# Gathers of a graph network in four forms: the same rows read as floats, as integer words, with an index bound, and as bytes

## What is computed

```python
def _gine_conv(x, src, dst, e, W1, b1, W2, b2):
    msg = relu(x[src] + e)                                # e: [E, 96], from the edge's weight
    agg = segment_sum(msg, dst, num_segments=N)
    h = relu((x + agg) @ W1 + b1)
    return relu(h @ W2 + b2)
# layer 0: two _gine_conv one after the other, then x = layernorm(x + h)
# layer 1: message = concat([x[row], x[col], edge_feat]), then relu(message @ W + b),
#          batch statistics over the edges, segment_sum by col; x = layernorm(x + agg + node_feat)
```

## Time and profile before

| | us |
|---|---|
| timed runs, median of 2 (12,207.96 and 12,225.78) | 12,216.87 |
| span of the profiled execution (the page gives no further time for it) | 14,691.4 |
| busy in it: PE / PEld | 9,543.3 / 6,790.2 |
| busy in it: POOL | 9,148.4 |
| busy in it: DVE / ACT | 7,533.7 / 4,925.7 |

### The profile page before, as it was taken

One profiled execution on the slowest core, in us unless ns is written; L12 is line 12 of the kernel. 1 busy time (PEld: TensorE's weight loads), 2 busy tenths in 40 slices (PEclk: granted clock), 3 DMA queues, 4 the chain that ended last, 5 costly groups with the idle time before them and its releaser, 6 DMA issues. The chain is left out here.

```text
span 14691.4 us, 164775 instructions
## 1 busy us (share of the span) xinstructions
PE 9543.3 (65%) x34164; PEld 6790.2 (46%) x34164; DVE 7533.7 (51%) x15604; ACT 4925.7 (34%) x11020; POOL 9148.4 (62%) x9725
## 2 busy tenths in 40 slices
PE   3666666666666677777777777766555555555556
PEld 2544444444444444455555555544444444444444
DVE  3433434334333444455555555556666666666666
ACT  2322222222222333333333333333333333333333
POOL 6466666666666566666666666656666666666665
PEclk9999999999999655555555555555555555555555
DMA  3111111111111211122222222211122222212122
GB/s 80 32 40 40 40 41 40 41 40 40 41 40 40 54 42 43 43 47 45 46 46 46 47 46 45 47 43 41 42 45 43 44 43 44 44 44 44 43 44 47
DMA packets 580837, 647.55 MB, mean 44 GB/s; under 512 B 411208, under 2 KB 411689, under 8 KB 579722
## 3 DMA queue, kind: packets, MB, share of 16 engines
q0 software_dynamic: 309504, 476.02, 15.5%
q1 hardware_dynamic: 219142, 139.69, 3.9%
q10 hardware_dynamic: 51712, 27.54, 0.7%
HBM read 604.68 MB, written 39.43 MB: 44 GB/s over the span
## 5 line engine op out<-in xcount | busy, mean ns | idle before, releaser
L1309 PE MATMUL ps_pre<-w_e,conv_hid 97*128 97x96 f32 x12896 | 3268.4, 433 | 2144.1 <-DVE conv_part L600 1554.4
L1309 PEld LDWEIGHTS ps_pre<-w_e,conv_hid 97*128 97x128 f32 x12896 | 2873.9, 326 | 2886.6 <-issue 2393.8
L1309 PE MATMUL ps_pre<-last_w_q,last_hid 128*128 128x96 f32 x6448 | 1627.8, 432 | 1540.8 <-issue 935.3
L1309 PEld LDWEIGHTS ps_pre<-last_w_q,last_hid 128*128 128x128 f32 x6448 | 1440.1, 327 | 1928.3 <-issue 1605.6
L264 POOL DMA_INDIRECT early_got<-in_x_rows,early_idx x1612 | 1524.3, 946 | 960.5 <-issue 439.0
L264 POOL DMA_INDIRECT early_got<-h_rows,early_idx x1612 | 1520.8, 943 | 944.2 <-issue 478.3
L264 POOL DMA_INDIRECT early_got<-p_rows,early_idx x1612 | 1520.4, 943 | 926.6 <-issue 463.3
L264 POOL DMA_INDIRECT last_got<-p_rows,early_idx x1612 | 1520.8, 943 | 905.0 <-issue 430.5
L264 POOL DMA_INDIRECT conv_got<-h_rows,early_idx x1612 | 1520.8, 943 | 884.0 <-issue 435.6
L264 POOL DMA_INDIRECT conv_got<-in_x_rows,early_idx x1612 | 1520.7, 943 | 853.1 <-issue 447.1
L582 ACT ACTIVATE conv_part<-ps_pre 128x384 bf16<-128x384 f32 x1736 | 816.0, 470 | 3676.9 <-DVE ps_pre L641 2405.4
(11 more groups left out here) (255 smaller groups left out, 10572.7 us busy)
## 6 DMA issues: line engine op xcount, KB each, us to landing
conv_row<-ea_parts SPq DMA_DIRECT2D x372, 84.5 KB
last_row<-ea_parts SPq DMA_DIRECT2D x372, 84.5 KB
early_got<-in_x_rows,early_idx POOLq DMA_INDIRECT x1612
conv_got<-in_x_rows,early_idx POOLq DMA_INDIRECT x1612
early_got<-h_rows,early_idx POOLq DMA_INDIRECT x1612
conv_got<-h_rows,early_idx POOLq DMA_INDIRECT x1612
early_got<-p_rows,early_idx POOLq DMA_INDIRECT x1612
last_got<-p_rows,early_idx POOLq DMA_INDIRECT x1612
```

Source lines behind the costliest of these rows:

```text
L1309: mm = pe.matmul(ps["pre"][q % 2][:, t * C:(t + 1) * C], hid[q % 2][0:P if last else C1, t * P:(t + 1) * P], w_q[j % U][:, c * C:(c + 1) * ...
```

## The change

Three more functions stand beside `gather`. `gather_words` reads both the table and the destination as 32-bit integers; `gather_checked` is the plain form with a bound on the index, 12,799, beyond which a row would be skipped without an error; `gather_bytes` reads both sides as bytes, so that a row is 384 elements rather than 96. Each moves the same 384 bytes a row. In `gpsimd_windows` slab j of a round is gathered by form[j]: slab 0 as before, slab 1 as words, slab 2 with the bound, slab 3 as bytes. `Preparation.gathers` keeps the plain form.

```diff
+U8 = mybir.dt.uint8
...
         def gather(gp, table, to, index, t, sem):
             gp.indirect_dma_start(to[:, t * C:(t + 1) * C], None, table, bass.IndirectOffsetOnAxis(index[:, t:t + 1], 0)).then_inc(sem, 16)
+
+        def gather_words(gp, table, to, index, t, sem):
+            gp.indirect_dma_start(to[:, t * C:(t + 1) * C].bitcast(I32), None, table.bitcast(I32),
+                                  bass.IndirectOffsetOnAxis(index[:, t:t + 1], 0)).then_inc(sem, 16)
+
+        def gather_checked(gp, table, to, index, t, sem):
+            gp.indirect_dma_start(to[:, t * C:(t + 1) * C], None, table, bass.IndirectOffsetOnAxis(index[:, t:t + 1], 0),
+                                  bounds_check=NPAD - 1, oob_is_err=False).then_inc(sem, 16)
+
+        def gather_bytes(gp, table, to, index, t, sem):
+            gp.indirect_dma_start(to[:, t * C:(t + 1) * C].bitcast(U8), None, table.bitcast(U8),
+                                  bass.IndirectOffsetOnAxis(index[:, t:t + 1], 0)).then_inc(sem, 16)
+
+        form = [gather, gather_words, gather_checked, gather_bytes]
...
                                 for i, t in enumerate(range(*group_tiles(g))):
                                     if near:
                                         close(k, NC_ * j + g, i)
-                                    gather(gp, table, got[j], idx[j], t, s[f"got{j}{g}"])
+                                    form[j](gp, table, got[j], idx[j], t, s[f"got{j}{g}"])
```

## The result

The changed kernel took 12,338.32 us (two runs, 12,336.70 and 12,339.93) against 12,216.87: a ratio of 1.0103, interval [1.0084, 1.0122]. That is 121 us more, inside the 2% band around no change and inside the forecast's range, but beyond the noise of the runs: the interval does not hold 1. What can be compared is every duration.

The account below looks back on a forecast made before the run. POOL's gather rate was taken as the bound: 9,672 x 1.248 = 12,071 us floor, 146 below the median. Words, bytes and bound added 0 + 0 + 0, so 12,217 us was forecast, range 12,110 to 12,640.

Parts of the forecast that it names:

- the MOVE: POOL's queue, ahead of each bounded gather: instruction putting the bound in a register, taken as covered by 1.25 us spacing, 0.
- rival 4: All gathers: forms differ by less than 0.1 us, nothing measurable; inside the forecast's 12,120 to 12,320, no chance of its own.
- the pauses: Whole core idle between gathers: 2,571 us of POOL pauses and waits, taken as belonging to the profiled execution, not timed runs.
- the distance of 1.248 us: POOL, start to start of gathers: 0.94 us busy plus 0.30 issue; 9,672 of them give a floor of 12,071 us.
- five waits of 221 us: POOL: 87.8 us in the first pass, 20.6, 23.6 and 17.1 around pass changes, 72 after the last gather.
- Rival 2: Byte gathers: 384-element rows are dearer; 12,580 us with a 0.15 us surcharge, 19,070 if rows are cut in four; chance 0.07.
- rival 3: One new gather form takes a shorter path, 0.84 us rather than 0.944, saving 242 us, time 11,975; chance 0.12.
- rival 1: Slab 2's 2,418 gathers: the explicit bound costs POOL 0.10 to 0.31 us each, 12,580 at the middle price; chance 0.18.
- The 0.10 us taken from the row of MEMSET: Bounded gathers: price if the comparison is a pass of its own over 128 lanes on POOL, +242 us.
- the rule of the Trainium skill: Bounded gathers: about 102 cycles per index fetched by itself, 10.9 us a gather, some 26,000 us; given no chance.
- the sum line: Whole kernel: form costs 0 + 0 + 0, profiled execution unchanged at 14,691 us, timed median 12,217 us.
- 7.4 ns a row: POOL's gather: 944 ns for 128 rows read as work going by rows, used to price dearer forms.

Follow-up runs that it names:

- e12: Kernel before with all four slabs bounded, bound loaded in a register once a pass, on a chip without pauses: 12,713.34 us against 12,210.33, ratio 1.0412.
- e11: Kernel before with slabs of 96 rows plain, 96 bounded, 32 plain, 32 bounded after each pass's first round: 11,887.02 us against 12,209.87, ratio 0.9736, one run.
- e10: Kernel before, all gathers plain, without the throttle waits of `close`, on a chip without pauses: 12,208.15 us against 12,209.87, ratio 0.9999.
- e2: Kernel before with words in slabs 0 and 2, bytes in 1 and 3, no bound, on a chip with pauses: 14,878.17 us against 14,877.60, ratio 1.0001.
- e3: Kernel before with all four slabs bounded, bound loaded in a register once a pass, on a chip with pauses: 14,859.60 us against 14,877.60, ratio 0.9988.
- e1: Kernel before with all four slabs bounded, a MOVE ahead of each bounded gather, on a chip with pauses: 14,974.24 us against 14,877.60, ratio 1.0066.
- e5: Kernel before with slabs of 128 rows plain, 128 bounded, 64 plain, 64 bounded after each pass's first round: 14,906.61 us against 14,843.74, ratio 1.0042, one run.
- e6: Kernel before with slab 0 plain, others bounded by 12,799 with error, 6,400 and 1, after each pass's first round: 14,938.88 us against 14,843.74, ratio 1.0064, one run.
- e7: Kernel before with all four slabs bounded, a MOVE per bounded gather, repeated on another chip with pauses: 14,928.95 us against 14,843.74, ratio 1.0057.
- e0: Kernel before, unchanged, with a new profile, on a chip with pauses: 14,882.43 us against 14,877.60, ratio 1.0003.

## Why the prediction was right

GpSimd's rate as the limit was right, and so were the costs of 0 for words, bytes and the MOVE. The price of 0 for the index bound was not, and the time lies inside the range because the range reached to 12,640 for a dearer bound. What came is rival 4, forms that differ by less than 0.1 us; but 12,338 is 18 us above the 12,320 given for it, and it does differ from no change beyond the noise.

- **The bound was POOL's rate, and a cost there is paid in full.** Right, and shown: 121 of 128 us in the change, 503 of 510 in e12, 323 of 335 in e11. The argument from the two times, that a run of 12,217 us leaves no room for the pauses, was what carried it. One step beside it was off: the distance of 1.248 us was taken to be 1% too long, because five waits of 221 us didn't fit beside it. Without pauses the distance is the same 1.249 us (e10); it is the wait of 87.8 us that isn't there, and the two changes of pass take 56 to 61 us.
- **Words and bytes cost nothing.** Right: 943 to 945 ns in the profile after and in e2, 32 packets a gather as before. Rival 2 (bytes dearer) and rival 3 (a shorter path) did not come.
- **The bound costs nothing.** Off in size: it costs 53 ns a gather, +128 us by the sum, where the forecast took 0 and rival 1 began at +0.10 us. This is the whole distance between 12,217 and 12,338. The reason given, one fixed routine in which the bound is a value, was wrong: a gather without a bound is shorter by 53 ns. The 0.10 us taken from the row of MEMSET lay above it, but that is luck: nothing shows that the comparison is a pass over the lanes. The range's lower end, 12,110, was said to take in -0.05 us on one form; that would be 12,096. What the rule of the Trainium skill in "GPSIMD Engine Reference", section "Performance pitfalls for Q7 kernels", would have made of an index fetched by itself, an estimated 10.9 us, is not seen in any form.
- **The MOVE is covered.** Right, by e3 and e12 against e1 and the change: 997 ns with it and without, the same gap, and no time without pauses. On chips with pauses 9 to 14 ns are paid for each (e1, e5, e6, e7), which the step did not foresee.
- **The pauses belong to the profiled execution.** As it was meant, of that one execution, this step failed. They are there in ten timed runs of e0 (14,878 to 14,888 us), and the profile after has none: its span is 12,334.9 us where the sum line said 14,691 unchanged, and its windows hold 291 gathers where the signs said 245 to 248. The prediction had two numbers, 14,691 and 12,217, and put the difference on profiling, when another reading, two chips, was open. Whether recording makes the pauses on some chips remains open, as said at e0. The step did no harm only because the result was measured without pauses. On one with them the same change would have paid less: e1 and e7, with four times as many bounded gathers, 0.6%.
- **7.4 ns a row.** This failed too. 863 of 944 ns are there with 32 rows. Rivals 1 and 2 priced their dear ends by it (+2.8 us for a row cut in four), and those ends were far too high.

## What to carry to other kernels

A gather of 32 to 128 rows of 384 bytes costs GpSimd about the same (within 9%) whatever its rows, their type, or how many a bound skips, so where GpSimd's rate sets the time it is mostly the number of gathers that counts, and an index bound that can't be reached should be left out: on every gather it is 4% of this kernel. Read a cost from the durations first and then ask whether it is paid; the same 53 ns were worth 503 us on one chip and nothing on another. When a profile's span and the timed median differ by a fifth, profile again before saying which of them the profile is about, and look whether the page gives landing times: where they are missing, so are semaphore events, and a wait put down to "issue" may have had a cause that wasn't recorded.

## What was not expected of the hardware

- One kernel has two times, 12,210 us on two chips and 14,844 and 14,878 us on two others, each repeated within 0.2%. In the longer one the gathers pause some 1,100 times, at the same TensorE clock (0.667 and 0.666 in the mean) and with the same time in queue 0, and the trace holds under a third of the semaphore events. The cause is open.
- An indirect DMA's time on GpSimd is nearly all fixed: 863 ns at 32 rows, 944 at 128. Its bound adds 38 to 53 ns, the error report 13 more, and skipped rows save none and appear still to be read from HBM.
